# Whole-tile transfers for the first rows and values, two stores for the last tiles, and a reordered start in a one-core attention and expert layer

## The reference

```
x = x + wkv(w, u, k = layernorm(x), v = ctx)        # a recurrence over the 128 steps
x = x + ffn(layernorm(x))
  # ffn: gates = softmax(x @ gate_w + gate_b), top 2 of 16 experts (512 -> 128 -> 512, gelu),
  #      plus two shared experts (512 -> 2048 -> 512, gelu), biases everywhere
```

## Time and profile before

| | us |
|---|---|
| median of three runs | 861.72 |
| the profiled execution: its own time | 862.01 |
| the profiled execution: span from first to last instruction | 860.4 |
| TensorE busy | 836.6 (97%) |
| VectorE busy | 617.8 (72%) |
| ScalarE busy | 467.2 (54%) |
| GpSimd busy | 236.9 (28%) |

### The profile page before, as it was taken

One profiled execution on the slowest core, in us unless ns is written; L12 is line 12 of the kernel. 1 busy time (PEld: TensorE's weight loads), 2 busy tenths in 40 slices (PEclk: granted clock), 3 DMA queues, 4 the chain that ended last, 5 costly groups with the idle time before them and its releaser, 6 DMA issues.

```text
span 860.4 us, 14380 instructions
## 1 busy us (share of the span) xinstructions
PE 836.6 (97%) x4102; PEld 693.1 (81%) x4102; DVE 617.8 (72%) x1244; ACT 467.2 (54%) x824; POOL 236.9 (28%) x277
## 2 busy tenths in 40 slices
PE   3889999999999999999999999999999999999998
PEld 2767888888888888888888888888888889998886
DVE  7787898977787778677787787576787544443684
ACT  6477866454476554445656464345555355656432
POOL 3100000134200000234000003232342488854870
PEclk9999999999999999999999999999999999999999
DMA  9913644389443332796443324867798388878977
GB/s 235 296 31 98 158 136 134 99 165 217 99 121 93 100 103 86 170 233 147 98 120 91 98 84 149 165 127 214 199 251 218 114 264 268 272 212 273 311 230 225
DMA packets 130144, 144.24 MB, mean 168 GB/s; under 512 B 11010, under 2 KB 89402, under 8 KB 129568
## 3 DMA queue, kind: packets, MB, share of 16 engines
q1 hardware_dynamic: 117792, 108.88, 48.7%
q0 software_dynamic: 11344, 33.50, 13.5%
q10 hardware_dynamic: 944, 1.07, 0.4%
HBM read 120.43 MB, written 22.98 MB: 167 GB/s over the span
## 4 chain that ended last, share of the span: by engine, by line
PE 93%; issue 0%; DVE 0%
PE up L640 13%; PE up L642 13%; PE up L641 13%; PE acc L701 13%; PE acc L703 13%; PE acc L707 13%; PE up L885 5%; PE acc L640 1%; PE acc L642 1%; PE acc L641 1%; PE misc L666 1%; PE up L666 1%; PE acc L811 1%; PE misc L719 1%; PE up L803 1%; PE misc L727 0%
## 5 line engine op out<-in xcount | busy, mean ns | idle before, releaser
L640 PE MATMUL up<-xs,w1hi 128*128 128x512 f32 (+1 forms) x512 | 198.6, 388 | 0.0
L642 PE MATMUL up<-xs,w1lo 128*128 128x512 f32 (+1 forms) x512 | 195.6, 382 | 0.0
L641 PE MATMUL up<-xs,w1hi 128*128 128x512 f32 (+1 forms) x512 | 195.6, 382 | 0.0
L963 ACT ACTIVATE hhi<-up,b_col 128x512 fp32r<-128x512 f32 x128 | 86.4, 675 | 200.1 <-PE up L642 161.2
L701 PE MATMUL acc<-w2hi,hhi 128*128 128x512 f32 x486 | 189.8, 391 | 0.1
L703 PE MATMUL acc<-w2lo,hhi 128*128 128x512 f32 x486 | 189.4, 390 | 0.0
L1239 DVE TENSOR_TENSOR hlo<-hf,hhi 128x512 fp32r<-128x512 f32 x128 | 85.5, 668 | 68.3 <-ACT hhi L963 28.7
L707 PE MATMUL acc<-w2hi,hlo 128*128 128x512 f32 x486 | 130.7, 389 | 0.0
L642 PEld LDWEIGHTS up<-xs,w1lo 128*128 128x128 f32 x512 | 96.3, 188 | 18.8
L640 PEld LDWEIGHTS up<-xs,w1hi 128*128 128x128 f32 x512 | 96.3, 188 | 18.6 <-issue 0.5
L641 PEld LDWEIGHTS up<-xs,w1hi 128*128 128x128 f32 x512 | 96.3, 188 | 17.7
(11 more groups left out here) (270 smaller groups left out, 1124.8 us busy)
## 6 DMA issues: line engine op xcount, KB each, us to landing
w_raw<-in_L_ffn_sw SPq DMA_DIRECT2D x256, 256.0 KB, 3.2
expert_rows<-ysb SPq DMA_DIRECT2D x47, 256.0 KB, 4.0
xn_rows<-kn POOLq DMA_DIRECT2D x16, 256.0 KB, 7.9
e2raw<-in_L_ffn_ew SPq DMA_DIRECT2D x16, 256.0 KB, 6.9
ew_sb<-in_L_ffn_ew SPq DMA_DIRECT2D x16, 256.0 KB, 7.4
X<-in_x SPq DMA_DIRECT2D x12, 256.0 KB, 7.8
vin<-in_ctx SPq DMA_DIRECT2D x12, 256.0 KB, 11.3
out<-X SPq DMA_DIRECT2D x12, 256.0 KB, 4.4
```

The costliest lines, as they stand in the source:

```text
L640: nc.tensor.matmul(o, lhs[0], rhs[0], start=start, stop=False)
L641: nc.tensor.matmul(o, lhs[0], rhs[1], start=False, stop=False)
L642: return nc.tensor.matmul(o, lhs[1], rhs[0], start=False, stop=stop)
L963: nc.scalar.activation(hhi[:, slot, tok], up[slot][:, tok], ACT.Gelu, bias=bias).then_inc(h_hi, 1)
```

## The change

Four things change. (1) Each of the tiles 0 to 3 of the first rows and of the first values is loaded by one transfer of 128 rows (256 KB) in place of four of 32 rows (64 KB), or, for tiles 2 and 3 together, four of 128 KB; each tile now has a semaphore of its own. (2) Each of the last four tiles is stored by one transfer of 64 rows from SyncE and one of 64 rows from ScalarE's queue, in place of two and two of 32 rows. (3) VectorE applies the first normalization before `tables()`, and ScalarE computes `first_keep` after `first_grow` and `early_exp(0)`. (4) `result_T(1)` moves from n = 4 to n = 0, `early_x(1)` from n = 6 to n = 5, and ScalarE's order around gelus 5 to 8 changes.

```
-        tabs0 = Steps(sem("tabs0"), "keep grow boost")
+        tabs0 = Steps(sem("tabs0"), "grow keep boost")
...
-        RESULT_AT = {4: 1, 8: 2, 14: 3}
-        X_AT = {6: 1, 10: 2, 16: 3}
+        RESULT_AT = {0: 1, 8: 2, 14: 3}
+        X_AT = {5: 1, 10: 2, 16: 3}
...
-            def load_tiles(tiles):
-                rows = slice(tiles[0], tiles[-1] + 1)
-                for g in range(GB):
-                    sp.dma_start(X2[32 * g:32 * g + 32, 0, rows], xq[0, g, :, rows]).then_inc(x_tile[tiles[0]], 16)
-
-            def load_values(tiles):
-                rows = slice(tiles[0], tiles[-1] + 1)
-                for g in range(GB):
-                    sp.dma_start(vin[32 * g:32 * g + 32, rows], vq[0, g, :, rows]).then_inc(v_tile[tiles[0]], 16)
+            def load_tile(i):
+                sp.dma_start(X2[:, 0, i], xq[0, :, :, i]).then_inc(x_tile[i], 16)
+
+            def load_value_tile(i):
+                sp.dma_start(vin[:, i], vq[0, :, :, i]).then_inc(v_tile[i], 16)
...
-            load_tiles([0])
-            load_tiles([1])
-            load_tiles([2, 3])
-            load_values([2, 3])
+            for i in range(TB):
+                load_tile(i)
+            for i in range(HT, TB):
+                load_value_tile(i)
...
-                for g in (0, 1):
-                    sp.dma_start(outq[NQ - 1, g, :, t], X2[32 * g:32 * g + 32, NQ - 1, t]).then_inc(out_done, 16)
-            sp.wait_ge(out_done, 16 * GB * (NQ - 1 + TB))
+                sp.dma_start(outq[NQ - 1, 0:2, :, t], X2[0:64, NQ - 1, t]).then_inc(out_done, 16)
+            sp.wait_ge(out_done, 16 * (GB * (NQ - 1) + 2 * TB))
...
             for i in range(HT):
-                for g in range(GB):
-                    act.dma_start(vin[32 * g:32 * g + 32, i], vq[0, g, :, i]).then_inc(v_tile[i], 16)
+                act.dma_start(vin[:, i], vq[0, :, :, i]).then_inc(v_tile[i], 16)
...
-            first_keep()
             first_grow()
             early_exp(0)
+            first_keep()
             first_boost()
...
-            for n in range(5):
+            for n in range(6):
                 pre_gelu(n)
-            for n in range(5, 7):
-                pre_gelu(n)
-                table_relu(n + 2)
-            pre_gelu(7)
+            for b in (7, 8):
+                table_relu(b)
+            pre_gelu(6)
             nc.scalar.preload_act_table_set("natural_log_exp_and_others")
             early_reciprocal(2)
             x_full(1)
             early_exp(3)
+            pre_gelu(7)
             pre_gelu(8)
...
-                for g in (2, 3):
-                    act.dma_start(outq[NQ - 1, g, :, t], X2[32 * g:32 * g + 32, NQ - 1, t]).then_inc(out_done, 16)
+                act.dma_start(outq[NQ - 1, 2:4, :, t], X2[64:128, NQ - 1, t]).then_inc(out_done, 16)
...
             early_ln1(0)
+            early_ln1_apply(0)
             tables()
-            early_ln1_apply(0)
             early_ln1(1)
```

More of the change, by code:

```diff
@@ L757, in value_T @@
             def value_T(i):
-                pe.wait_ge(v_tile[min(i, 2)], 16 * GB)
+                pe.wait_ge(v_tile[i], 16)
                 for k in range(KC):
@@ L1289, in early_ln1 @@
             def early_ln1(i):
-                dve.wait_ge(x_tile[min(i, 2)], 16 * GB)
+                dve.wait_ge(x_tile[i], 16)
                 early_stats(early1, i)
@@ L1656, in _ @@
             early_ln1_apply(1)
-            dve.wait_ge(x_tile[2], 16 * GB)
+            dve.wait_ge(x_tile[2], 16)
             V.bn_stats(st6[:, 2], X2[:, 0, 2]).then_inc(early1.sem, 1)
```

## The result

| | before | changed |
|---|---|---|
| median of four executions | 861.75 | 886.86 (886.47 to 888.07) |
| the profiled execution's own time | 862.01 | 887.04 |
| its span | 860.4 | 884.9 |

The ratio of the medians is 1.0292, 95% interval 1.0279 to 1.0306: slower by 2.9%, against 2.6% predicted. In the changed kernel L517 and L520 load rows and values on SyncE's queue, L1060 values on ScalarE's, L627 and L1202 are the last stores; L755 is `value_T`, L766 `result_T`, L1376 and L1381 the end of `early_result` and `early_add`, L806 the early down product, L635 the main loop's first product.

What follows compares the result with a forecast made beforehand. TensorE bounds the main loop, so only prologue and last stores can change; 8.4 + 17.8 - 4.1 = 22.1 takes the profiled 862.01 to 884.1, the median 0.3 lower: 883.8 us, 80% range 871.5 to 891.

Steps and rivals of the forecast that it cites:

- loads on 4 engines: Prologue: whole-tile loads run on 4 DMA engines, last values land at 26.1 us, `result_T(0)` late; 8.4 us lost.
- stores on 2 engines: Kernel end: the last stores run on 2 shared DMA engines and drain until 877.4 us; 17.8 us lost.
- order of the products: Before the main loop: result 1 transposed at n = 0 removes most of TensorE's 4.8 us idle; 4.1 us gained.
- normalization ahead of tables: Prologue, VectorE and ScalarE: nothing while late loads cover it, near zero without; bounds -0.5 and +0.5 us.
- Which engines: First loads, last stores: outermost count of either side limits the engines, 4 and 2, the same for both queues.
- The price of a packet: Loads and stores: 0.09 us per 2 KB packet on one engine (0.085 to 0.10), so 23.0 us for 256 packets.
- The cover of result 0: Prologue: result 0 comes at about 23 us instead of 18.49, still ahead of the last values at 26.1.
- Part 1: TensorE from 33.67 to 67.77 us: the new order of products leaves 0.7 of 4.8 us idle; 4.1 us gained.
- Part 3: Prologue: kn 0.6 us earlier, grow and boost as much later; zero under late loads, within 0.5 us without.
- faster rival: Whole-tile loads and stores use all 16 engines, cut by the 128 partitions: 857.3 us; chance 0.13.
- Different engines for the two queues: Loads and stores: each queue has its own engines, so 865 us, or 872 with only stores apart; chance 0.05.
- No effect: Whole edit: the removed wait returns at gelu 7 and the whole-tile transfers cost little: 861.7 us; chance 0.02.

Runs made afterwards that it cites:

- stores-back: Changed kernel with only its last stores cut back into transfers of 32 rows, whole-tile loads kept: 869.77 us, ratio 1.0088.
- both-back: Changed kernel with first loads and last stores both cut back to transfers of 32 rows, new order of work kept: 859.99 us, ratio 0.9978.
- loads-back: Changed kernel with only its first loads cut back into transfers of 32 rows, changed stores kept: 877.33 us, ratio 1.0176.
- old order with finer loads: Normalization-back kernel with the old order of products restored too, one semaphore a tile kept: 862.75 us, ratio 0.9975.
- normalization-back: Both-back kernel with the old normalization order (tables() and first_keep first) restored too: 858.87 us, ratio 0.9956.
- pairs of sequences: Changed kernel with stores of 32 rows and each tile loaded in two transfers of two sequences (64 rows): 891.61 us, ratio 1.0300.
- results in the middle: Normalization-back kernel with results 2 and 3 transposed between up and down product of n = 7 and n = 13: 859.78 us, ratio 0.9940.

## Why the prediction was right, and where its terms were off

The change was slower, by two transfers that run on few engines, as forecast, and 886.86 lies in the range of 871.5 to 891. The terms, in us:

| step | predicted | measured | where |
|---|---|---|---|
| loads on 4 engines | +8.4 (7.1 to 10.9) | +8.95 | `result_T(0)`; stores-back less both-back: 9.0 |
| stores on 2 engines | +17.8 (16.6 to 20.4) | +18.16 | after the last add; loads-back less both-back: 18.2 |
| order of the products | -4.1 (3.3 to 4.8) | -2.94 | 2.9 against the old order of the kernel before, 1.9 against the old order with finer loads |
| normalization ahead of tables | 0 (-0.5 to +0.5) | nothing seen here (no run isolates it), +1.1 without its cover | both-back less normalization-back |
| main loop, and outside the span | 0 | +0.9 | the profiled execution |

**Which engines: right.** The choice between the cut by 128 partitions and the cut by the outermost count was the one that decided the sign, and it was taken from eight packets. The packet count came out as forecast to the unit (264), the busy shares are those of 4 and 2 engines, and the pairs of sequences, slower with smaller transfers, shut the door on the other reading. The Trainium skill's rule (*DMA: Bandwidth & Descriptors*, "Why a DMA increments its semaphore by 16 and not by 1"), the largest number up to 16 that divides the slowest dimension of both sides, gives 4 for the loads and 2 for the stores and for the pairs; the traces agree, at 100, 50 and 50 GB/s with busy shares of 0.26, 0.13 and 0.13. Its other half, that SyncE's and ScalarE's transfers use the lowest-numbered engines and so the same ones, agrees with the run that put one queue's half of the stores back; no trace here gives the engines' numbers.

**The price of a packet: sizes that offset each other.** A 2 KB packet on one engine takes 2048 B / 25.2 GB/s = 0.081 us by the flat stretches, below the 0.09 taken and below its lower end of 0.085. The rates are 100 and 50 GB/s where the prediction had 92 and 46. The 23.0 us of each part would be 20.7. The terms came out near nonetheless, and that is luck, since the engines are not full at once: the loads run at 32 and 72 GB/s in their first two microseconds and have the small vectors and the zero fill among them, and "the engines never pause" does not hold for the stores, which run at 11 to 36 GB/s for the six slices from 860.7 us (5.4 us) before they reach 50. From 861 to 863 us only ScalarE's queue moves packets, though both queues issued their first store at 859.97. What holds the stores back there stays open.

**The cover of result 0: thinner than forecast.** It was to be ready at about 23, and was at 26.69. ScalarE's copy of value tile 1 stands ahead of its part of the reciprocal and waits 4.68 us for the load, at 20.71; the prediction followed VectorE through the late x1, and left out that ScalarE stands behind the late values too. It also had the order of the landings wrong: it let the two queues share the engines, with v0 at 10.1, x1 at 12.3 and v1 at 16. The first uses of x1, v0 and v1 were at 10.68, 14.29 and 19.56. `value_T(3)`, at 26.59, still covered result 0: `result_T(0)` follows at 27.50, 0.8 us after its result.

**Part 1 was mis-sized by 1.2 us.** The prediction counted to 67.77, a row of the chain; the timeline has the first product at 67.50, so 4.5 us were idle and not 4.8. It left 0.7 of them; 1.6 were left. It had found that result 1 stood behind down products and took that away, and did not ask the same of results 2 and 3. Result 2 is transposed at 54.93 behind a down product, so VectorE idles 1.07 us before its add (1.09 at result 3), and TensorE then waits 0.37 us for `early_x(2)`; just before, it had waited 0.25 for gelu 7. Moving these two transpositions won 1.0 us of start in the run with results in the middle, which is most of the difference.

**Part 3: its price without the cover was wrong.** In the changed kernel it costs nothing that shows, since the values are later still. The boost table wasn't there a microsecond early, though: VectorE waits 0.47 us for it, until 14.60, and then 0.77 for the copy of value tile 0. The step that failed is "kn earlier by 0.6, grow and boost later by as much". `kn` was not earlier, because its input `rstd` was not: six small instructions were moved out of a wait that they had filled for nothing. And grow and boost were later by 0.3 and 1.3, the whole of it ahead of `early_h`. Measured, 1.1 us. This takes 1.1 us from the faster rival's gain as well, and the order of the products another 1.2: its 857.3 becomes 859.6, and the kernel with both transfers of 32 rows had 859.99.

**The rivals.** All 16 engines: refuted by 264 packets, 100 GB/s and the busy shares. Different engines for the two queues: refuted by the half put back. No effect: refuted. A whole tile in one transfer whose outermost count is 16 or more on both sides wasn't tried.

## What to carry to other kernels

Fewer and larger transfers are not the same as faster ones: look first at the outermost count of both sides of the transfer, since a view of 2 or 4 blocks ran at 50 or 100 GB/s here, while the many small transfers of before held SyncE's queue only 2.8 us longer for all the rows. The number of tiny packets on a queue tells how many engines took part, before anything is changed. When one transposition is moved out from behind a product, ask the same of its siblings; and before small work is moved behind a larger operation, see whether it had been running in that operation's wait.

## What the runs showed that was not expected

- The issue of a transfer is itself held up when few engines carry the backlog. SyncE took 8.38 us to issue two value tiles (0.7 each for the rows before them), and with pairs 21.66 us for eight transfers, so that everything behind on SyncE's queue starts later. The first row after it, the gate weights, was issued at 12.22.
- Few engines hurt the strangers on them as well. ScalarE's small vectors, issued at the same time as before, reach TensorE at 8.91 in place of 4.46. With only the loads back to 32 rows it is 4.38, so the whole-tile loads do it; that they do it by standing ahead on the same engines is the likely way, not shown.
- VectorE's scan and GpSimd's `boost` operation are slower when they overlap: 1.51 and 1.79 us (10.01 and 9.49 in the both-back kernel; 1.50 and 1.80 in the changed one), 1.26 and 1.50 where they hardly do. The Trainium skill (*SBUF — State Buffer*, "Who interferes with whom") says that a VectorE instruction with two SBUF inputs contends with a GpSimd one that reads SBUF, for a port pair that is an exclusive lock, by which the later one blocks for the whole of the other. By that the scan could not have ended before 9.49 + 1.50 + 1.26 = 12.25; it ended at 11.52. The profile's times on GpSimd are rough, but the rows show a slowing by 0.25 to 0.3 us, not a block; and where `es` lies wholly within GpSimd's operation (8.96 in 8.45 to 9.95, old normalization order), neither is slowed at all.
